# A Perceiver block on one core: compact key-value matrices, corrected in three groups of batches

## What is computed

```python
q = (decoder_seq @ Wq.T + bq).reshape(B, T_dec, N_HEADS, D_HEAD)
k = (encoder_seq @ Wk.T + bk).reshape(B, T_enc, N_HEADS, D_HEAD)
v = (encoder_seq @ Wv.T + bv).reshape(B, T_enc, N_HEADS, D_HEAD)
kv = jnp.einsum('bthd,bthe->bhde', k, v)
att = jnp.einsum('bqhd,bhde->bqhe', q, kv) * scale
return layer_norm(att + decoder_seq, ln_gamma, ln_beta)
```

## Time and profile before

| | us |
|---|---|
| median of 3 runs | 594.95 |
| lowest and highest run | 593.56, 595.21 |
| the profiled execution, its own time | 591.21 |
| its span, first to last instruction | 589.4 |
| PE busy (share of the span) | 574.4 (97%) |
| DVE, ACT, POOL busy | 351.5, 201.7, 221.2 |

### The profile page before, as it was taken

The page is one execution under the profiler, slowest core; times in us unless marked ns, Lnnn a source line. Parts: engine busy times, 40 slices in busy tenths (PEclk is TensorE's granted clock), DMA queues, the critical chain, the costliest instruction groups (busy, mean ns, idle before and its releaser), DMA issues.

```text
span 589.4 us, 11467 instructions
## 1 busy us (share of the span) xinstructions
PE 574.4 (97%) x4860; PEld 494.4 (84%) x4864; DVE 351.5 (60%) x410; ACT 201.7 (34%) x286; POOL 221.2 (38%) x182
## 2 busy tenths in 40 slices
PE   6999999999999999999999999999999999999997
PEld 6989888898989889797778988978888887888886
DVE  4887771826546182652597257567777446875741
ACT  3544343505234351513602451423341122434320
POOL 2599963565626265560325000203333543000000
PEclk9999999999999999999999999999999999999999
DMA  8763423141213324005102502206822421798601
GB/s 305 275 237 131 152 79 146 71 151 71 76 76 101 122 71 151 1 1 176 35 2 74 152 3 72 66 8 148 219 72 74 140 71 72 173 259 203 151 1 71
DMA packets 25284, 65.76 MB, mean 112 GB/s; under 512 B 2424, under 2 KB 2424, under 8 KB 22304
## 3 DMA queue, kind: packets, MB, share of 16 engines
q1 hardware_dynamic: 25248, 65.23, 35.7%
HBM read 64.05 MB, written 1.18 MB: 111 GB/s over the span
## 4 chain that ended last, share of the span: by engine, by line
PE 79%; DVE 6%; POOL 5%; issue 2%; ACT 1%; POOLq 0%; DVEq 0%
PE ps L317 16%; PE ps L319 15%; PE ps L318 15%; PE ps L823 8%; POOL psum_tmp L455 4%; PE ps L846 3%; PE ps L850 3%; PE ps L838 2%; PE ps L833 2%; PE ps L832 2%; PE ps L902 2%; PE ps L837 2%; DVE stats L1309 1%; PE ps L864 1%; PE ps L1113 1%
## 5 line engine op out<-in xcount | busy, mean ns | idle before, releaser
L455 POOL TENSOR_TENSOR psum_tmp<-psum_tmp,raw 128x512 f32<-128x512 f32 (+1 forms) x88 | 139.9, 1589 | 34.3 <-DVE lo L1336 25.8
L823 PE MATMUL ps<-hi 128*128 128x256 f32 (+3 forms) x416 | 129.7, 313 | 4.8 <-ACT hi L537 4.8
L823 PEld LDWEIGHTS ps<-hi 128*128 128x128 f32 (+1 forms) x416 | 78.9, 190 | 5.3 <-ACT hi L537 4.8
L1336 DVE TENSOR_TENSOR lo<-raw,hi 128x2048 fp32r<-128x2048 f32 (+1 forms) x29 | 61.7, 2159 | 24.4 <-ACT hi L529 24.4
L317 PE MATMUL ps<-hi,gh 128*128 128x512 f32 x192 | 75.7, 394 | 0.0
L319 PE MATMUL ps<-hi,gl 128*128 128x512 f32 x192 | 74.8, 390 | 0.0
L318 PE MATMUL ps<-lo,gh 128*128 128x512 f32 x192 | 74.8, 390 | 0.0
L510 POOL TENSOR_TENSOR sx<-sx,raw 128x512 f32<-128x512 f32 x32 | 41.0, 1290 | 82.3 <-DVE raw L1664 82.3
L710 ACT ACTIVATE hi<-raw 128x2048 fp32r<-128x2048 f32 x14 | 26.8, 1914 | 93.0 <-PE ps L319 83.6
L317 PE MATMUL ps<-wvh,gh 128*128 128x512 f32 x128 | 50.9, 398 | 0.0
L319 PE MATMUL ps<-wvh,gl 128*128 128x512 f32 x128 | 50.0, 391 | 0.0
(11 more groups left out here) (218 smaller groups left out, 1197.6 us busy)
## 6 DMA issues: line engine op xcount, KB each, us to landing
raw<-in_ctx SPq DMA_DIRECT2D x23, 1024.0 KB, 4.8
raw<-in_ve SPq DMA_DIRECT2D x8, 1024.0 KB, 5.3
raw<-in_oe SPq DMA_DIRECT2D x8, 1024.0 KB, 5.4
wk<-gm_rows SPq DMA_DIRECT2D x8, 512.0 KB, 9.1
g<-gm_rows SPq DMA_DIRECT2D x8, 512.0 KB, 9.7
raw<-in_ctx SPq DMA_DIRECT2D x8, 130.0 KB
xres<-in_x SPq DMA_DIRECT2D x1, 1024.0 KB, 9.8
mb<-in_WqT SPq DMA_DIRECT2D x1, 1024.0 KB, 13.5
```

What stands on the lines that cost most here:

```text
L455: pool.tensor_tensor(psum_tmp[0:k, :], (raw[:, 0, :] if t == 1 else psum_tmp[0:k, :]), raw[0:k, t, :], ALU.add).then_inc(ctx_sum, 1)
L823: pe.matmul(dst, hi[0:kk, t, cols], x, start=start and opens, stop=stop and closes, skip_group_check=True)
L1336: dve.tensor_tensor(lo[0:k, r, :], raw[0:k, r, :], hi[0:k, r, :].bitcast(F32), ALU.subtract).then_inc(ctx_lo, 1)
```

## The change

For the batches 0 to 6 the matrices stay compact. In place of `kv_copy`, DVE copies 128x128 (`kv_keep`) into the first 128 columns of `kv[:, b, :]`. The corrections come in three groups, batches 0 and 1, 2 and 3, and 4 to 6: `group_corrections(n)` copies the group's compact matrices into a bank by one product with the identity (256 or 384 columns), and adds 16 products of 64x32 weights by 64 or 96 columns, one for each head. The spreading by heads comes behind that: for group 0 on DVE (two of the old operations), for the groups 1 and 2 on ACT (`group_spread`, four scaled copies of 256 or 384 columns each).

The order is new as well. PE: `group_corrections(0)` ahead of `g_transposes(7)`; then `kv_part(6)`, `attend(0)`, `group_corrections(1)`, `m_part(7, 0)`, `attend(1)`, `group_corrections(2)`, `m_part(7, 1)`, `attend(2)`, `m_part(7, 2)` and `(3)`. ACT: `last_gh_high` makes the upper half first, the lower one once the transposes are there; `w_high(W_OUT, 1, 1)` moves up between the copies of `m_part(7, 1)` and `(7, 2)`. DVE: `group_spread(0)`, `last_gl_low`, then the token tiles, each `part1_residual` and `norm_back` one step earlier. POOL alternates `rstd_of(1, i)` and `rstd_of(2, i)`. SP's load of owT waits for the second group's corrections instead of `kv_part(7)`.

The diff, cut to its core:

```diff
+        groups = ((0, 2), (2, 4), (4, 7))
...
-            sp.wait_ge(kv_mm, B)
+            sp.wait_ge(r2_mm, 2)
             sp.dma_start(raw[:, half(1), :], blocks(a["owT"])).then_inc(ld_w[1], 16)
...
-            for b in range(4):
+            def last_gh_high():
+                act.wait_ge(m_mm, (B - 1) * 4)
+                act.wait_ge(gl_done, (B - 1) * 3)
+                act.wait_ge(g_add, B * 5)
+                act.activation(upper(ghf, 5 * P), upper(g32f, 5 * P), ACT.Copy).then_inc(gh_done, 1)
+                act.activation(last_block(ghf), last_block(g32f), ACT.Copy).then_inc(gh_done, 1)
+                act.wait_ge(gt_mm, B)
+                act.activation(lower(ghf), mir[:, 0:2, :].rearrange("p m n -> p (m n)")[:, 0:6 * P].rearrange("p (m n) -> p m n", m=3),
+                               ACT.Copy).then_inc(gh_done, 1)
+
+            def group_spread(n):
+
+                act.wait_ge(r2_mm, n + 1)
+                src = group_bank(n).rearrange("p (m d) -> p m d", d=D1)
+                dst = kv[:, groups[n][0]:groups[n][1], :].rearrange("p b (c j d) -> p (b c) j d", j=4, d=D1)
+                for j in range(4):
+                    act.activation(dst[:, :, j, :], src, ACT.Copy, scale=headmask[:, D1 * j:D1 * j + 1]).then_inc(r2_act, 1)
+
+            for b in range(3):
                 right_part(b)
             m_copy(B - 2, (3,))
-            gh_high(B - 1)
-            for b in range(4, B):
+            last_gh_high()
+            for b in range(3, 7):
                 right_part(b)
-            m_copy(B - 1)
+            group_spread(1)
+            m_copy(B - 1, (0,))
+            group_spread(2)
+            right_part(B - 1)
+            m_copy(B - 1, (1,))
+            w_high(W_OUT, 1, 1)
+            m_copy(B - 1, (2, 3))
...
+            def group_corrections(n):
+
+                first, end = groups[n]
+                if n == 0:
                     pe.wait_ge(bk_near, 1)
                     pe.wait_ge(rk_near, 1)
...
+                if n == 2:
+                    pe.wait_ge(gl_done, 3 * B)
+                pe.wait_ge(kv_done, end)
+                pe.matmul(group_bank(n), ident[:, :], kv[:, first:end, 0:P], start=True, stop=False, skip_group_check=True)
+                pe.wait_ge(rb_done, end)
+                at = group_bank(n).rearrange("p (b m) -> p b m", m=P)
                 for c in range(KC):
-                    cols = slice(c * P, (c + 1) * P)
-                    mm = pe.matmul(rank2_bank(b)[:, cols], left[:, cols], right_of(b)[:, cols], start=True, stop=True)
+                    for j in range(4):
+                        cols = slice(c * P + D1 * j, c * P + D1 * j + D1)
+                        mm = pe.matmul(at[D1 * j:D1 * j + D1, :, D1 * c:D1 * c + D1], left[:, cols], raw[0:64, 4 + first:4 + end, cols],
+                                       start=False, stop=True, skip_group_check=True)
                 mm.then_inc(r2_mm, 1)
...
+            group_corrections(0)
             g_transposes(B - 1)
             kv_part(B - 2)
-            for b in range(4):
-                rank2(b)
             attend(0)
+            group_corrections(1)
+            m_part(B - 1, 0, False)
             attend(1)
-            for b in range(4, B - 1):
-                rank2(b)
+            group_corrections(2)
+            m_part(B - 1, 1, False)
             attend(2)
...
-            for m in range(KC):
+            for m in range(2, KC):
                 m_part(B - 1, m, False)
-            pe.wait_ge(r2_done, B - 1)
...
+            def kv_keep(b):
+                dve.wait_ge(kv_mm, b + 1)
+                dve.tensor_copy(kv[:, b, 0:P], bank[6][:, 0:P]).then_inc(kv_done, 1)
...
-            for b in range(4):
-                rank2_add(b)
-            gl_upper(B - 1)
+            group_spread(0)
+            last_gl_low()
             part1_out(0)
-            rank2_add(4)
-            rank2_add(5)
+            part1_residual(0)
             part1_out(1)
-            rank2_add(6)
-            part1_residual(0)
+            norm_back(2, 0)
+            part1_residual(1)
             part1_out(2)
-            part1_residual(1)
-            norm_back(2, 0)
+            norm_back(2, 1)
             part1_residual(2)
-            norm_back(2, 1)
             norm_back(2, 2)
             xT_pair_low(1, 0, range(KC))
```

More of the change, by code:

```diff
@@ L164, in perceiver_block @@
             sem(s) for s in ("half_ones", "s_mm", "srow_done", "sT_mm", "s_done", "r_mm", "pick_done"))
-        bk_near, rk_near, rv_sum, right_near, rb_done, r2_mm, r2_done = (
-            sem(s) for s in ("bk_near", "rk_near", "rv_sum", "right_near", "rb_done", "r2_mm", "r2_done"))
+        bk_near, rk_near, rv_sum, right_near, rb_done, r2_mm, r2_dve, r2_act = (
+            sem(s) for s in ("bk_near", "rk_near", "rv_sum", "right_near", "rb_done", "r2_mm", "r2_dve", "r2_act"))
         att_mm, y_done, xb_done, z_done, x1_done, ob_done = (
@@ L264, in right_of, with group_bank @@
             return raw[0:64, 4 + b, :] if b < B - 1 else psum_tmp[0:64, :]
-        def rank2_bank(b):
-            return bank[(1, 2, 0, 4, 1, 2, 4)[b]]
+        groups = ((0, 2), (2, 4), (4, 7))
+        def group_bank(n):
+            return bank[(1, 2, 4)[n]][:, 0:P * (groups[n][1] - groups[n][0])]
         def by_tile(t):
@@ L479, in _ @@
                 pool.tensor_tensor(xres[:, i, :], xres[:, i, :], beta[:, :], ALU.add).then_inc(xb_done, 1)
[L480 to L485, removed]
+            for i in range(3):
+                rstd_of(1, i)
+                rstd_of(2, i)
             def add_out_b(i):
@@ L642, in _ @@
             xT_pair_high(1, 1)
-            w_high(W_OUT, 1, 1)
             for k in range(KC):
@@ L963, in sum_rows @@
                 mm.then_inc(r_mm, 1)
-            def rank2(b):
-                if b == 0:
+            def group_corrections(n):
+                first, end = groups[n]
+                if n == 0:
                     pe.wait_ge(bk_near, 1)
                     pe.wait_ge(rk_near, 1)
[L969 to L975, removed]
+                if n == 2:
[4 more added lines that the diff above has]
+                at = group_bank(n).rearrange("p (b m) -> p b m", m=P)
                 for c in range(KC):
-                    cols = slice(c * P, (c + 1) * P)
-                    mm = pe.matmul(rank2_bank(b)[:, cols], left[:, cols], right_of(b)[:, cols], start=True, stop=True)
+                    for j in range(4):
+                        cols = slice(c * P + D1 * j, c * P + D1 * j + D1)
+                        mm = pe.matmul(at[D1 * j:D1 * j + D1, :, D1 * c:D1 * c + D1], left[:, cols], raw[0:64, 4 + first:4 + end, cols],
+                                       start=False, stop=True, skip_group_check=True)
                 mm.then_inc(r2_mm, 1)
@@ L988, in attend @@
                     pe.wait_ge(right_near, 1)
-                pe.wait_ge(r2_done, min(2 * i + 2, B - 1))
-                if i == NT - 1:
+                if i == 0:
+                    pe.wait_ge(r2_dve, 2)
+                elif i < NT - 1:
+                    pe.wait_ge(r2_act, 4 * i)
+                else:
                     pe.wait_ge(kv_done, B)
@@ L1374, in gl_upper, with kv_spread @@
                 dve.tensor_tensor(last_block(glf), last_block(g32f), last_block(ghf).bitcast(F32), ALU.subtract).then_inc(gl_done, 1)
-            def kv_copy(b):
+            def kv_keep(b):
+                dve.wait_ge(kv_mm, b + 1)
+                dve.tensor_copy(kv[:, b, 0:P], bank[6][:, 0:P]).then_inc(kv_done, 1)
+            def kv_spread(b):
                 dve.wait_ge(kv_mm, b + 1)
@@ L1440, in _ @@
             gl_low(1)
-            kv_copy(0)
+            kv_keep(0)
             with dve.Fori(2, B - 1) as b:
@@ L1449, in _ @@
                 gl_low(b)
-                kv_copy(b - 1)
+                kv_keep(b - 1)
             for c in range(1, 4):
@@ L1472, in _, with group_spread, last_gl_low @@
             dve.tensor_tensor(by_tile(right), by_tile(right), near4(slice(0, 64)), ALU.mult).then_inc(right_near, 1)
[L1473 to L1480, removed]
+            def group_spread(n):
+                dve.wait_ge(r2_mm, n + 1)
+                for b in range(groups[n][0], groups[n][1]):
+                    m = b - groups[n][0]
+                    dve.tensor_tensor(by_head_of(kv[:, b, :]), spread_heads(group_bank(n)[:, m * P:(m + 1) * P]), near_heads,
+                                      ALU.mult).then_inc(r2_dve, 1)
+            def last_gl_low():
+                dve.wait_ge(gh_done, B * 3 - 1)
+                dve.tensor_tensor(upper(glf, 5 * P), upper(g32f, 5 * P), upper(ghf, 5 * P).bitcast(F32), ALU.subtract).then_inc(gl_done, 1)
+                dve.tensor_tensor(last_block(glf), last_block(g32f), last_block(ghf).bitcast(F32), ALU.subtract).then_inc(gl_done, 1)
+                kv_keep(B - 2)
+                dve.wait_ge(gh_done, B * 3)
```

(20 more changed lines are left out.)

## The result

| | us |
|---|---|
| before, median of 8 runs | 594.35 (590.51 to 595.76) |
| after, median of 8 runs | 589.37 (588.96 to 592.15) |
| ratio after to before | 0.9933, 95% interval 0.9909 to 0.9958 |
| profiled execution of after, its own time; span | 589.40; 587.6 |
| forecast | 591.7, range 589.4 to 593.7, against a median of 594.95 |

The account below looks back on a forecast made before the run. PE, busy 97% of the span, was taken to bound the kernel, with DVE's chain setting the changed stretch's end: 311.6 instead of 314.80, a gain of 3.2 us, so 594.95 - 3.2 = 591.7 us, range 589.4 to 593.7.

Parts of the forecast that it names:

- PE's path: PE from 287.79 us to the end of kv_part(7) with corrections: 310.2, with shape changes 310.8, against 314.55; gain 3.7 us.
- their lower bound: Small products of one group of corrections on PE: 0.46 us if the count of instructions decides.
- the late chain: Rival: DVE's token-tile work waits for last_gl_low and slips 1 to 1.5 us; gain 1.9 us, 593.1; chance 0.15.
- PE's work: Corrections on PE: 6.9 us of rank2 removed, three groups of 0.96, 0.96 and 1.44 added; 3.5 us less to do.
- Both rivals with the products in a row: Group corrections on PE: no overlap across column groups, 596.2, chance 0.04; weight loads not overlapping, about 600, chance 0.02.
- the stretch: PE's timeline from the end of m_part(6, 3) to transposes_1(2), before at 287.79 to 314.80 us; almost all PE work.
- DVE has no reserve: At the low half of G, ready 292.9 us with PE there at 292.85; all token-tile work queues behind last_gl_low.
- DVE's chain sets the time: Token tiles on DVE from 292.9 to 311.6 us; PE, there at 310.8, waits 0.8 us; gain 3.2 us.
- The contention of root and norm_back: POOL's root and DVE's norm_back go one after the other: 3.4 us per middle tile; chance 0.45.
- the rival without it: Root and norm_back don't block each other; PE doesn't wait at the end; gain 4.0 us, 590.9; chance 0.27.
- Edits at nothing: kv_keep in the loop, ACT's group_spread(1) and (2), early owT load and split, POOL's order: costed at nothing.
- the whole difference passes through: Behind transposes_1(2), at 314.80 us before: what reaches that point earlier comes out fully at the end.

Follow-up runs that it names:

- a_slow: Changed kernel plus one 128x512 subtraction (0.68 us) on DVE in last_gl_low, ahead of the lower low half of G; median 591.58 us, ratio 0.9972 to the kernel before.
- a_front: Changed kernel plus 8 small products (16 in the trace) at the very front of PE's program; median 591.80 us, ratio 0.9976 to the kernel before.
- a_pool: Changed kernel with POOL's first addition of out_b held until the third norm_back; median 590.98 us, ratio 0.9941 to the kernel before.
- b0: The kernel before, run and profiled once more without any edit; median 594.52 us, ratio 1.0018 to the kernel before.
- b_port: The kernel before, with POOL's additions of beta held until DVE has masked `right`; median 593.17 us, ratio 0.9986 to the kernel before.
- a_owt: Changed kernel with owT loaded behind kv_part(7) and split behind the transposed tiles, as before the change; median 590.62 us, ratio 0.9942 to the kernel before.
- a_together: Changed kernel with the four parts of batch 7 together behind attend(2), not interleaved; median 597.35 us, ratio 1.0041 to the kernel before.
- a0: The changed kernel, run and profiled once more without any edit; median 590.79 us, ratio 0.9935 to the kernel before.

## Why the prediction was right, and where not

**The time.** The forecast of faster held. 589.37 lies at the range's lower edge, 0.03 us below it; from the median with which the forecast was made the ratio gives 594.95 x 0.9933 = 591.0, inside. The saving was forecast as 3.2 us and is 4.0 (2.5 to 5.4). Part of that agreement is chance: steps missed and their errors went both ways, as told below. Two sums of the forecast don't come out of their rows. PE's path adds up to 310.1, not 310.2. And the lower edge of the range, 4.7 us of gain, should be 4.0 and the 0.3 by which the small products get cheaper at their lower bound, so 4.3 and an edge of 589.9. The upper edge, the late chain with the scatter of 0.8, should be 593.9 instead of 593.7.

**PE's work** held in kind. The small products overlap across the column groups: 18 ns each with 64 columns, 25 with 96, where I took 15 and 22. The three groups cost 3.95 us instead of 3.4. Both rivals with the products in a row are out, that of the Trainium skill (TensorE: Matmul & The Clock Gate, "Part 3: Packing small matmuls — row/col tiling") too. All the weight loads of a group go to the same rows, and a load and its product pass in 18 ns.

**Fetching instructions** was not in the sum at all, but for a word under the late chain. It put 1.16 us into `kv_part(6)`: with it the stretch is 25.0 us, without it 23.7, against my 23.8. That 23.7 and 23.8 are so close is chance too: mine holds 0.9 us of contention that isn't there, and lacks 0.55 us of groups and DVE's wait for `attend(2)`. The late chain is what this looks like, with PE late instead of DVE.

**"DVE has no reserve", and DVE's chain sets the time**: wrong. DVE waited 0.36 and 0.75 us for `attend(1)` and `attend(2)`, and a_slow took 0.68 us from it without making the stretch longer. I let the chain start at 292.9 and did not wait for the attentions, as I put `attend(1)` at 297 and `attend(2)` at 302.4 to 303. They ended near 298.6 and 304.2, by the wait for instructions and by 0.5 us of groups. In a_front, without the wait for instructions, DVE no longer waits for `attend(1)`, but still 0.57 us for `attend(2)`. What sets the end is PE up to `attend(2)`, and DVE's tail behind it.

**The contention of root and norm_back**: wrong, the rival without it was right. I counted 3.4 us for a tile with its norm_back; it was 3.01. The root took 1.07 us beside both, against 1.02 beside the scaling alone: POOL waits once, for the scaling, and norm_back adds nothing to it and keeps its 0.54 us. But norm_back beside POOL's wide additions does take 1.5 instead of 0.55 us (a_pool), as I had read from the row. So the lock that the Trainium skill names (SBUF — State Buffer, "Who interferes with whom") fits the scaling and the wide additions; between a root of one element per partition and norm_back no trace here shows it.

**What before waits for.** I read 0.23 us ahead of `kv_part(6)` and said that it now has cover. In b0 it is 1.02 us, and that is hidden as well, by the cover and by the scaled copy that ACT makes later: 0.8 us of gain that one profile did not show. By the same section of the Trainium skill (SBUF — State Buffer, "Who interferes with whom") the masking, with two inputs in SBUF, is just such an operation, and who starts first keeps the port; the rows under b0 and b_port agree.

**Edits at nothing.** owT: nothing, by a_owt. ACT's spreading has cover, and a_together says what it would cost without: two waits of 1.78 and 2.12 us and the clock behind them, 6 us of stretch in all. My line said only that the parts cover it.

**From stretch to total.** I assumed that the whole difference passes through, and it does. From the end of the stretch to the end of the span the executions with a mean clock of 0.997 take 274.6 us in before and 274.8 in after; b0, a0 and a_pool, at 0.994, take 276.3, 276.5 and 276.7. The stretch is 2.0 us shorter between the first two profiles and 2.7 between b0 and a0, and at equal clock the time falls by 2.9 to 3.2. Yet the profiled a0 is only 1.0 us below b0: it came to the stretch 1.5 us later (288.72 against 287.24), 0.4 of it by a longer wait in `kv_part(5)` (1.33 against 0.96), and the rest from other differences ahead of the change. The 4.0 of the result has an interval from 2.5 on, so there may be nothing left to explain; whether the clock has a share in it stays open.

## What to carry to other kernels

Fewer PE instructions are worth their time only if what feeds the next step stands behind other PE work: the same compact products gave 0.65% in one order and cost 1.6% in another (four runs). Before taking one profile for the kernel, look at a second: a wait that reads 0.23 us in one reads 1.0 in the next. When a chain on another engine seems to set the end, check at each step whether it waits for the engine that you are relieving.

## What I had not expected of the hardware

- PE stood up to 2.8 us in waits named issue, and each of the 34 in these profiles ended 1.2 to 1.6 us behind the landing of a 16 KB packet of an instruction queue. The place in `near_values` is fixed in the stored program: 16 products more ahead, even ahead of the loop, moved it by exactly 16. The waits stood among dense small products (`kv_part` at 10 ns each, `near_values` at 31, group products at 18), in `half_norms` and once in `attend(3)`. The length differs between executions of the same place: 0 to 1.7 us in `kv_part(5)`.
- Behind waits of 1.8 and 2.1 us, close together, PE was at 1.2 GHz for part of 12 us (0.72 of the clock); that cost some 3 us beside the 3.9 of the waits.
- A DVE operation on 64x512 elements with both inputs in SBUF took 0.68 us when it started before POOL's addition of 128x512, and 1.6 to 1.7 when it started behind it; in the first case POOL's addition took 1.75 us instead of 1.29.
